# Another order of the steps in a decoder's windowed attention, on all four engines that share it

## What is computed

```python
HEADS, KV_HEADS, HEAD_DIM, WINDOW = (16, 4, 128, 64)
q, k, v = heads(x @ Wq.T), heads(x @ Wk.T), heads(x @ Wv.T)
q, k = _rms_norm(q, qn_w), _rms_norm(k, kn_w)
q, k = q * cos + _rotate_half(q) * sin, k * cos + _rotate_half(k) * sin
q = q * Dh ** (-0.5)
scores = einsum('bhgtd,bhkd->bhgtk', q, k)          # 4 query heads per key head
scores = where((dist >= 0) & (dist <= WINDOW), scores, min)
ctx = einsum('bhgtk,bhkd->bhgtd', softmax(scores), v)
x = x + ctx @ Wo.T
```

## Time and profile before

| what | value |
|---|---|
| median of 3 runs | 1577.93 us (1576.06 to 1578.44) |
| the profiled execution's own time | 1575.46 us |
| its span, first to last instruction | 1573.5 us |
| mean granted TensorE clock | 0.930 |
| busy share PE, DVE, ACT, POOL | 85%, 68%, 53%, 39% |
| windowed stage, from its first scores to its last sum | 733 to 1221 us, about 31% of the span |

### The profile page before, as it was taken

One profiled execution on the slowest core, in us unless ns is written; L12 is line 12 of the kernel. 1 busy time (PEld: TensorE's weight loads), 2 busy tenths in 40 slices (PEclk: granted clock), 3 DMA queues, 4 the chain that ended last, 5 costly groups with the idle time before them and its releaser, 6 DMA issues. The chain is left out here.

```text
span 1573.5 us, 26789 instructions
## 1 busy us (share of the span) xinstructions
PE 1342.1 (85%) x8144; PEld 1050.8 (67%) x8144; DVE 1066.7 (68%) x2064; ACT 828.4 (53%) x1851; POOL 608.6 (39%) x687
## 2 busy tenths in 40 slices
PE   5885488886899999956899989989997889888998
PEld 4663255554788888844777767777776556556887
DVE  4789688887366666668777777777776466653443
ACT  4431388887544353426666656666665355552332
POOL 1100755565640000008665666666565433320000
PEclk9897699999899999977999999999999799998999
DMA  7000633330000000002000000000000000000000
GB/s 280 1 0 1 214 94 80 80 80 14 1 1 1 1 0 0 1 1 97 1 1 0 0 0 0 0 0 0 0 1 0 6 3 3 3 2 1 14 14 27
DMA packets 30736, 40.26 MB, mean 26 GB/s; under 512 B 4368, under 2 KB 25872, under 8 KB 29264
## 3 DMA queue, kind: packets, MB, share of 16 engines
q1 hardware_dynamic: 30672, 39.45, 8.2%
HBM read 28.96 MB, written 2.10 MB: 20 GB/s over the span
## 5 line engine op out<-in xcount | busy, mean ns | idle before, releaser
L1773 ACT ACTIVATE wi_weights<-wi_psum,wi_bias,wi_scale 128x128 f32<-128x128 f32 x256 | 113.7, 453 | 114.5 <-DVE wi_bias L1883 114.5
L1548 POOL TENSOR_TENSOR wi_straight<-wi_straight,wi_crossed 128x512 f32<-128x512 f32 x80 | 109.9, 1374 | 5.8 <-DVE wi_crossed L1869 5.7
L915 DVE TENSOR_REDUCE gq_top<-gq_psum 128x4 f32<-128x512 f32 x128 | 86.9, 679 | 33.4 <-PE gq_psum L802 32.5
L1536 POOL TENSOR_TENSOR wi_scratch<-wi_sums,wi_eps 128x4 f32<-128x4 f32 x80 | 36.1, 452 | 158.3 <-DVE wi_sums L1852 157.0
L869 ACT ACTIVATE gq_weights<-gq_weights 128x512 f32<-128x512 f32 x128 | 81.1, 634 | 26.9 <-DVE gq_weights L923 25.6
L1874 DVE TENSOR_REDUCE wi_top<-wi_psum 128x4 f32<-128x512 f32 x64 | 44.0, 688 | 73.4 <-PE wi_psum L1663 73.4
L809 PE MATMUL gq_psum<-const,gq_weights 128*128 128x128 f32 x512 | 79.1, 278 | 15.0 <-ACT gq_weights_t L875 14.9
L1087 POOL TENSOR_TENSOR ex_scratch<-ex_squares,ex_eps 128x4 f32<-128x4 f32 x12 | 2.4, 199 | 229.6 <-ACT ex_junk L1198 229.6
L1211 ACT ACTIVATE ex_hidden_high<-ex_gated 128x512 fp32r<-128x512 f32 x64 | 40.4, 632 | 92.7 <-DVE ex_gated L1284 92.7
L1284 DVE TENSOR_TENSOR ex_gated<-ex_gated,ex_psum 128x512 f32<-128x512 f32 x64 | 43.9, 686 | 64.1 <-PE ex_psum L1139 53.6
L923 DVE TENSOR_TENSOR gq_weights<-gq_psum,gq_top 128x512 f32<-128x512 f32 x128 | 87.3, 682 | 0.0
(11 more groups left out here) (344 smaller groups left out, 4101.2 us busy)
## 6 DMA issues: line engine op xcount, KB each, us to landing
gq_keys<-in_ctx_keys_dram SPq DMA_DIRECT2D x16, 512.0 KB, 3.7
gq_keys_diagonal<-gq_key_parts SPq DMA_DIRECT2D x64, 128.0 KB, 3.8
x<-in_x_dram SPq DMA_DIRECT2D x4, 512.0 KB, 7.8
gate<-in_gate_dram SPq DMA_DIRECT2D x2, 1024.0 KB, 5.4
up<-in_up_dram SPq DMA_DIRECT2D x2, 1024.0 KB, 7.4
down<-in_down_dram SPq DMA_DIRECT2D x2, 1024.0 KB, 9.4
wq<-in_wq_dram SPq DMA_DIRECT2D x1, 2048.0 KB, 8.4
wo<-in_wo_dram SPq DMA_DIRECT2D x1, 2048.0 KB, 10.6
```

Of the source, the lines that this page charges most:

```text
L915: dve.tensor_reduce(top[:, u % 4, :], rows(u), AX.X, ALU.max).then_inc(topped, 1)
L1548: added_up = pool.tensor_tensor(straight[:, at], straight[:, at], crossed[:, at], ALU.add)
L1773: act.activation(weights[:, g % 2, j, :], ps[:, SC + g % 2, j * P:j * P + P], ACT.Exp, bias=bias[:, g % 2, j:j + 1], scale=scale[:, g, j:j ...
```

## The change

It writes the units in another order, on every engine:

- PE: scores first, then the weights' transposes, all projections, the heads' transposes, the weighted sums, and the output projection last.
- `ahead`: the next row's k is projected in unit 1 where it was in unit 2, and v in unit 2 where it was in unit 1; the first row's too, and the pieces of Wk are made ready before those of Wv.
- DVE: `maximum`, `shift`, then `take_weights`; `finish` goes from unit 1 to unit 2 and ahead of `invert`; all `rotate` come behind `invert`; the sums of squares are a step of their own, `add_squares`, and come last. In unit 0 `normalise` comes behind `maximum`, and `split_h` ahead of `split_out`.
- ACT: `weigh` first, then the copies of projections, turned heads, `take_attended`, and the squares (`take_square`) last.
- POOL: `normalise` first, then the queries' `join`, every `find_scale`, and a key's `join` last.

No instruction is added or taken away but for register arithmetic. The core of the diff:

```diff
-            following = [[], [("v", 0)], [("k", 0), ("q", 0)], [("q", 1)]][g] if not last else []
+            following = [[], [("k", 0)], [("v", 0), ("q", 0)], [("q", 1)]][g] if not last else []
...
                 for g in range(U):
                     items = [item for item in ahead(t, s, g, last) if item[0] != "v"]
-                    for item in items[:1]:
+                    normalise(t, g)
+                    for item in items:
+                        if item[0] == "q":
+                            join(*item)
+                    for item in items:
                         find_scale(*item)
-                    normalise(t, g)
-                    for item in items[:1]:
-                        join(*item)
-                    for item in items[1:]:
-                        join(*item)
-                        find_scale(*item)
+                    for item in items:
+                        if item[0] == "k":
+                            join(*item)
...
                 for g in range(U):
-                    items = ahead(t, s, g, last)
-                    for item in items:
-                        if item[0] != "v":
-                            project(*item)
                     scores(t, s, g)
-                    for item in items:
-                        if item[0] == "v":
-                            project(*item)
                     if g > 0 or not first:
                         pt, _, pg = earlier(t, s, g, 1, U)
                         turn_weights(pt, pg)
-                    if g > 1 or not first:
-                        pt, _, pg = earlier(t, s, g, 2, U)
-                        project_out(pt, pg)
-                    if g > 0 or not first:
-                        attend(*earlier(t, s, g, 1, U))
+                    for item in ahead(t, s, g, last):
+                        project(*item)
...
+                    if g > 0 or not first:
+                        attend(*earlier(t, s, g, 1, U))
+                    if g > 1 or not first:
+                        pt, _, pg = earlier(t, s, g, 2, U)
+                        project_out(pt, pg)
...
-                    for item in ahead(t, s, g, last):
+                    items = ahead(t, s, g, last)
+                    weigh(t, g)
+                    for item in items:
                         take(*item)
-                    weigh(t, g)
-                    if g > 0 or not first:
-                        pt, _, pg = earlier(t, s, g, 1, U)
-                        take_attended(pt, pg)
...
+                    if g > 0 or not first:
+                        pt, _, pg = earlier(t, s, g, 1, U)
+                        take_attended(pt, pg)
+                    for item in items:
+                        if item[0] != "v":
+                            take_square(*item)
...
                 for g in range(U):
+                    items = ahead(t, s, g, last)
+                    maximum(t, g)
                     if g == 0 and not last:
                         normalise(t + 1, 1 - s)
-                    maximum(t, g)
+                    shift(t, g)
                     if g > 0 or not first:
                         pt, _, pg = earlier(t, s, g, 1, U)
                         take_weights(pt, pg)
-                    shift(t, g)
-                    items = [item for item in ahead(t, s, g, last) if item[0] != "v"]
-                    for item in items[:1]:
+                    if g == 2 and not first:
+                        finish(t - 1)
+                    invert(t, g)
+                    for item in items:
                         rotate(*item)
-                    invert(t, g)
-                    for item in items[1:]:
-                        rotate(*item)
-                    if g == 1 and not first:
-                        finish(t - 1)
+                    if g == 0 and not last:
+                        split_h(t + 1, 1 - s)
                     if g > 0 or not first:
                         pt, _, pg = earlier(t, s, g, 1, U)
                         split_out(pt, pg)
-                    if g == 0 and not last:
-                        split_h(t + 1, 1 - s)
+                    for item in items:
+                        add_squares(*item)
```

More of the change, by code:

```diff
@@ L1397, in windowed @@
 def windowed(nc, net, sem):
-    PIECES = ["v", "k", "q0", "q1", "q2", "q3", "o0", "o1", "o2", "o3"]
-    LOW_BY_DVE, LOW_BY_POOL = ["v", "k", "q0", "q1", "o2", "o3"], ["q2", "q3", "o0", "o1"]
+    PIECES = ["k", "v", "q0", "q1", "q2", "q3", "o0", "o1", "o2", "o3"]
+    LOW_BY_DVE, LOW_BY_POOL = ["k", "v", "q0", "q1", "o2", "o3"], ["q2", "q3", "o0", "o1"]
     U = KVH
@@ L1486, in ahead @@
             own = [("q", t, s, g + 2)] if g < 2 else []
-            following = [[], [("v", 0)], [("k", 0), ("q", 0)], [("q", 1)]][g] if not last else []
+            following = [[], [("k", 0)], [("v", 0), ("q", 0)], [("q", 1)]][g] if not last else []
             return own + [(what, t + 1, 1 - s, head) for what, head in following]
-        FIRST_ITEMS = [("v", 0, 0, 0), ("k", 0, 0, 0), ("q", 0, 0, 0), ("q", 0, 0, 1)]
+        FIRST_ITEMS = [("k", 0, 0, 0), ("v", 0, 0, 0), ("q", 0, 0, 0), ("q", 0, 0, 1)]
         def of_six(what, t, g):
-            return 6 * t + {"v": 0, "k": 1, "q": 2 + g}[what]
+            return 6 * t + {"k": 0, "v": 1, "q": 2 + g}[what]
         def of_five(what, t, g):
@@ L1575, in _ @@
                 take_low(pool, name, low_pool)
-            find_scale(*FIRST_ITEMS[1])
-            for item in FIRST_ITEMS[1:]:
-                join(*item)
+            find_scale(*FIRST_ITEMS[0])
+            for item in FIRST_ITEMS:
+                if item[0] != "v":
+                    join(*item)
                 if item[0] == "q":
@@ L1640, in project @@
                 need(pe, proj_taken, n - 1)
-                if what == "v":
+                if what == "k":
                     pe.wait_ge(turned_taken, number("h", t) + 1)
@@ L1740, in take, with take_square @@
                 if what == "k":
-                    need(act, parts, 3 * (of_five("k", t - 1, 0) + 1))
+                    used = of_five("k", t - 1, 0) + 1
                 else:
-                    need(act, parts, 3 * (of_five("q", t, g - 2) + 1) if g >= 2
-                         else 3 * (of_five("q", t - 1, g + 2) + 1))
+                    used = of_five("q", t, g - 2) + 1 if g >= 2 else of_five("q", t - 1, g + 2) + 1
+                need(act, parts, 3 * used)
+                need(act, squared, used)
                 act.activation(raw[:, at].rearrange("p j d -> p (j d)"), bank, ACT.Copy).then_inc(proj_taken, 1)
+            def take_square(what, t, s, g):
+                n, at = of_five(what, t, g), slot(what, g)
                 act.wait_ge(proj_taken, of_six(what, t, g) + 1)
@@ L1839, in split_out, with add_squares @@
                                   ALU.subtract).then_inc(out_low_ready, 1)
-            def rotate(what, t, s, g):
+            def add_squares(what, t, s, g):
                 if what == "v":
@@ L1853, in rotate @@
                                   ALU.add).then_inc(summed, 1)
+            def rotate(what, t, s, g):
+                if what == "v":
+                    return
+                at = slot(what, g)
+                dve.wait_ge(proj_taken, of_six(what, t, g) + 1)
                 if what == "k":
```

## The result

The changed kernel takes 1584.97 us (median; 1580.59 to 1587.13), the kernel before in the same session 1577.3 us: a ratio of 1.0049, 95% interval 1.0036 to 1.0061. It is slower by some 8 us, which is inside the range, on the side to which the prediction gave 0.51, and 4 us above the predicted 1581. The profiled execution took 1584.97 us with a span of 1583.2.

The account below looks back on a forecast made before the run. PE's 2.7 us wait for wi_out_low goes, but DVE's loop is as long as the row. Steady rows +1.3, start +1.2, last row +1.2, end -0.5 make +3.2, or 1581.1 us on the median; range 1560 to 1602.

Parts of the forecast that it names:

- The steady row: Rows 1 to 14: a row takes 30.7 us against 30.63 before, +1.3 us over 14 rows.
- Unit 0: DVE's loop in unit 0: 6.47 plus normalise 0.2, split_h 0.4 and the row's end 0.3, making 7.35 us.
- Unit 2: DVE's loop in unit 2: queuing in turns with POOL's scales and key work adds 1.05, making 7.5 us.
- The start: Up to row 1: key's scale found 1.4 us later, first bias held up by POOL anyway; +1.2 us.
- The last row's +1.2: Last row's three units: 18.1 us where they took 16.88, the one without a rotation set by PE at 5.2.
- Behind the last maximum: End of the stage: the last bias no longer stands behind a copy, -0.5 us.
- the cost of the slow clock: PE in the kernel before: half speed loses 1.8 us a row; without it and the wait, PE needs 26.2.
- That POOL's power holds DVE up: Rival: POOL's power locks out DVE's bias, 2.1 us a row, 1611 us in all; chance 0.03.
- That PE's clock stays low: Rival: PE's clock stays low and PE becomes the bound, 32.0 us a row at 0.82, 1599 us; chance 0.20.
- Better turns of DVE and POOL: Rival: k's products and POOL's key work in units 1 and 2 fall better, row 28.6, 1552 us; chance 0.15.
- That the normalise would not hold the rotation: Rival: POOL's normalise doesn't hold DVE's rotation up, PE sets the row at 26.6, 1525 us; chance 0.05.
- the signs named: In every unit, queries' cos products take 1.3 us and the reciprocal waits over 1 us for ACT, among others.

Follow-up runs that it names:

- e3: Changed kernel, but POOL's normalise multiplies only the first column of each head's weights: 1547.44 us, ratio 0.9809 to the kernel before.
- e2: Changed kernel, but in units 0, 1 and 3 the first item is copied before the exponentials and rotated before the reciprocal: 1565.39 us.
- e5: Changed kernel, but DVE does the low part and the previous unit's squares (except unit 1's) before the reciprocal, POOL's scales a unit later: 1557.09 us.
- e1: Kernel before, with only PE's output projection moved to the end of a unit: 1588.47 us, ratio 1.0081 to the kernel before.
- e7: Changed kernel, but the prologue sums the first items' squares before rotating them: 1583.13 us, a single execution.
- e4: Kernel before, but POOL's normalise multiplies only the first column of each head's weights: 1554.57 us, ratio 0.9869 to the kernel before.
- e8: Kernel before, but DVE rotates every item behind the reciprocal and POOL normalises first: 1632.2 us, ratio 1.0356 to the kernel before.
- e6: Changed kernel, but v is projected in unit 1 and k in unit 2 as before, and POOL joins the key before the query: 1621.93 us.

## Why the prediction was right

**The sign and the mechanism held.** The prediction said that the wait for wi_out_low goes, that DVE's loop is as long as the row was, and that nothing is gained. The waits show it, and e3, e2 and e5 bear it out: each shortens DVE's loop by another means and each shortens the row, while e1, which takes PE's wait away with DVE's order kept, does not. The change took 2.68 us of idle time and some 1.6 us of slow clock off PE in each row, and the row did not get shorter. That the sign came out has luck in it: it was a call at 0.51, and 0.1 us in a unit is worth 5.6 us.

**The steady row, +1.3 predicted, +3.7 measured.** Unit 3 was put at 6.47 and took 6.44, unit 1 at 9.4 and took 9.50. Unit 0 was put at 7.35 and took 7.10 in the row shown and 7.03 in the mean: of the 0.3 for the row's end 0.1 shows, between the bias and the first exponential (988.31 to 988.62, where unit 3 has 981.66 to 981.86). Unit 2 was put at 7.5 and took 7.94, and this is the step that failed in size. I had the query's cos product start 3.55 behind the maximum; it starts at 3.78, since ACT copies v out ahead of the query, so that DVE stands 0.80 for the raw query. And I had the sin products end at 6.4; they end at 6.83, as their 2.44 us stand behind two of POOL's instructions, the key's scaling (976.84, 1.54 us, itself held up by the cos product) and the normalise (978.34). The row came to 30.89 for the predicted 30.72; it would have missed by more if unit 0's excess had not covered most of unit 2's, and that is luck.

**The start, +1.2 predicted, +4.4 measured.** It lies outside the bounds that I gave, -2 and +4. I had counted the late scale of the key once, as 1.4 us; e7 shows 3.9: 3.1 up to the first maximum, and 0.8 behind it, as it also let POOL's split of Wo go ahead of the first bias. I had taken that bias to be held up either way, by the 1.93 us of the earlier trace rows; it took 2.30, and in e7 it was not held up at all.

**The ends.** The last row's +1.2 was met (18.13 for the predicted 18.1). Behind the last maximum it was -2.0 for -0.5; how much of that is the change's I did not test.

**PE's clock.** I put the cost of the slow clock at 1.8 us a row and PE's own need at 26.2, from the mean of 0.94. e4 has PE's order of the kernel before at both levels: the rows at 1.00 are 1.56 us shorter than those at 0.94, and PE is busy 26.45 us in them for 28.00. So 1.8 was 0.2 too much, and at full clock the kernel before needs PE for some 26.4 us a row. What I missed is that the new order needs more: at a granted clock of 1.00 PE is busy 321.84/367.65 x 30.89 = 27.0 us a row with the change, and in e5 356.86/380 x 28.93 = 27.2. Why, no run shows. In the sum this cost nothing; in e5, where the row came down to 28.93, the maximum waits for scores again.

**What the parts are worth.** The output projection alone costs 0.87 us a row (e1), the late rotation alone 3.45 (e8), and the earlier key is worth 2.64 in the changed kernel (e6). That makes +1.7 where the whole change has +0.26, so the parts do not simply add up. The scores ahead of the projections, ACT's order and the squares at the unit's end were not run alone.

**The rivals.** That POOL's power holds DVE up fell: the bias at 973.72 took 0.16 beside the power at 972.93. By the Trainium skill ("SBUF — State Buffer", section "SBUF: two separate sides") it would have been held; the trace disagrees for this power of 128x4 as it did before. That PE's clock stays low fell as well, with 1.00 granted. Better turns of DVE and POOL did not come. That the normalise would not hold the rotation fell by e3. Of the signs named, two hold only in three units of four: in unit 2 the query's cos product is 0.69, and the reciprocal waits 0.44, since `finish` stands in its wait.

## What to carry to other kernels

When engines with fixed queues pass work round in a loop, take the loop of each engine through the others and sum it, idle waits included, before you remove a stall from one of them: here PE lost a stall of 2.7 us and the half speed behind it, and DVE's loop was as long. Work that does not need the awaited answer belongs in the time for which an engine waits for it: moving the rotation out of the exponentials' time cost 3.45 us a row in the kernel before, and moving two other pieces into it won 1.96 in the changed one. And look at each row of the loop and not at the mean alone: in e4 the mean clock of 0.96 was made up of rows at 1.00 and rows at 0.94.

## What was not expected

- The length of the gap ahead of it does not settle PE's clock. With idle time of 2.68 us ahead of the output projection every row of the kernel before had 0.94, and with the changed kernel's longest of 1.66 every row had 1.00, though PE had less to do. But in e4 the idle time was 1.94 to 1.99 in every row, and eight rows of fourteen had 0.94 and six 1.00; in e1 the longest was 1.51 to 1.52 in every row, and three of fourteen had 0.95 and took 32.75 us for 31.15. What decides in these rows no run shows.
- A vector instruction of 128x4 is also held up by a large POOL one. In e5 the bias at 859.99 took 0.55 us beside a join of 128x512 at 859.24, where 0.15 is usual; beside the power of 128x4, 1.01 us long, it took 0.16. DVE's size is the same in both. Whether it is POOL's size or its operation that decides, no run shows.
- The reverse holds for POOL: beside DVE's cos product at 850.18 in e5, POOL's addition of 128x4 took 0.65 us (850.87) for the usual 0.20.
